# Four pipelined loops of a two-layer transformer kernel written out in full

## The reference, cut to what matters

```python
# layer 0 (per sequence; cond gives scale and shift)
h = film(rmsnorm(x, norm1_w), cond, film1_w, film1_b)
Q, K, V = h @ q_w + q_b, h @ k_w + k_b, h @ v_w + v_b          # one head, 256 wide
x = x + softmax(Q @ K.T * 256**-0.5) @ V @ proj_w + proj_b
h = film(rmsnorm(x, norm2_w), cond, film2_w, film2_b)
x = x + gelu(h @ mlp_w1 + mlp_b1) @ mlp_w2 + mlp_b2             # 256 -> 1024 -> 256
# layer 1
cmod = silu(c) @ w_ada + b_ada                                  # six vectors per sequence
k, q, v = split(modulate(ln(x)) @ w_qkv)                        # 16 heads of 16 channels
x = x + gate_msa * (softmax(q @ k.T / 16) @ v @ w_proj + b_proj)
x = x + gate_mlp * (gelu(modulate(ln(x)) @ w_mlp1 + b_mlp1) @ w_mlp2 + b_mlp2)
```

## Time and profile before

| | |
|---|---|
| timed runs, median (lowest to highest) | 1570.15 us (1569.04 to 1573.56) |
| profiled execution / its span | 1573.3 / 1571.3 us |
| PE busy | 97% of the span, 14186 matmuls |
| weight loads (PEld) | 87% |
| DVE, ACT, POOL busy | 81%, 57%, 32% |
| granted TensorE clock, mean | 0.995 of full speed |
| DMA | 148.55 MB, mean 95 GB/s |
| chain that ended last | PE 78%, DVE 8%, SPq 7%, DMA 3%, issue 2% |

### The profile page before, as it was taken

The page is one execution under the profiler, slowest core; times in us unless marked ns, Lnnn a source line. Parts: engine busy times, 40 slices in busy tenths (PEclk is TensorE's granted clock), DMA queues, the critical chain, the costliest instruction groups (busy, mean ns, idle before and its releaser), DMA issues.

```text
span 1571.3 us, 42207 instructions
## 1 busy us (share of the span) xinstructions
PE 1518.1 (97%) x14186; PEld 1361.8 (87%) x14186; DVE 1275.0 (81%) x2826; ACT 891.7 (57%) x1813; POOL 499.5 (32%) x647
## 2 busy tenths in 40 slices
PE   8999999999999998899999999999998999999999
PEld 7999998999999998666777777777766999999999
DVE  5798888787777778788888888888885888888886
ACT  3566664444444453677777777777777344444443
POOL 2333332010000013366655666655644300000000
PEclk9999999999999999999999999999999999999999
DMA  5700002211111111444444434434432233232332
GB/s 177 220 21 20 20 20 63 77 43 48 46 53 47 47 50 54 142 132 133 140 132 133 137 130 134 141 127 138 133 117 75 80 99 101 93 95 93 100 100 68
DMA packets 167663, 148.55 MB, mean 95 GB/s; under 512 B 24528, under 2 KB 146448, under 8 KB 167584
## 3 DMA queue, kind: packets, MB, share of 16 engines
q1 hardware_dynamic: 167424, 147.47, 29.6%
q0 software_dynamic: 160, 0.04, 0.1%
HBM read 62.61 MB, written 32.41 MB: 60 GB/s over the span
## 4 chain that ended last, share of the span: by engine, by line
PE 78%; DVE 8%; SPq 7%; DMA 3%; issue 2%; ACT 1%; DVEq 0%; ACTq 0%
PE bank L216 60%; PE bank L1755 6%; SPq L1695 4%; DVE C_negmax L1767 4%; PE bank L1793 3%; PE bank L1811 3%; SPq L2118 2%; DMA C_qs<-C_mT 2%; PE bank L1821 2%; PE bank L1829 1%; PE bank L415 1%; PE bank L793 1%; PE bank L488 1%; SPq L287 1%; PE bank L198 1%
## 5 line engine op out<-in xcount | busy, mean ns | idle before, releaser
L1767 DVE TENSOR_REDUCE C_negmax<-bank 128x4 f32<-128x1024 f32 x248 | 303.3, 1223 | 75.4 <-PE bank L1755 74.5
L1901 ACT ACTIVATE C_probs<-bank 128x1024 f32<-128x1024 f32 x256 | 262.5, 1025 | 111.3 <-PE bank L1793 106.7
L374 POOL TENSOR_TENSOR m_small<-m_small,consts 128x2 f32<-128x2 f32 x64 | 48.2, 753 | 573.9 <-DVE m_small L368 290.3
L1129 ACT ACTIVATE B_g<-bank,B_bias 128x256 f32<-128x256 f32 x256 | 107.4, 471 | 196.7 <-PE bank L216 196.4
L1129 ACT ACTIVATE D_g<-bank,D_bias 128x256 f32<-128x256 f32 x256 | 107.3, 472 | 190.9 <-PE bank L216 190.7
L1755 PEld LDWEIGHTS bank<-C_kx,C_qs 64*128 64x128 f32 x1024 | 80.8, 193 | 90.0 <-DVE C_negmax L1767 60.5
L1755 PE MATMUL bank<-C_kx,C_qs 64*128 64x256 f32 x1024 | 128.2, 328 | 21.5 <-DMA C_qs<-C_q_lo 8.0
L216 PE MATMUL bank<-B_wt_w_hi,B_g_lo 128*128 128x256 f32 x512 | 143.0, 279 | 3.5 <-DVE B_g_lo L1139 3.4
L216 PE MATMUL bank<-D_wt_w_hi,D_g_lo 128*128 128x256 f32 x512 | 142.3, 278 | 3.3 <-DVE D_g_lo L1139 3.3
L216 PE MATMUL bank<-D_wt_w_lo,D_g_hi 128*128 128x256 f32 x512 | 141.8, 277 | 0.0
L216 PE MATMUL bank<-D_wt_w_hi,D_g_hi 128*128 128x256 f32 x512 | 141.8, 277 | 0.0
(11 more groups left out here) (270 smaller groups left out, 4909.2 us busy)
## 6 DMA issues: line engine op xcount, KB each, us to landing
C_qs<-C_q_hi SPq DMA_DIRECT2D x128, 128.0 KB
C_kx<-C_k_hi SPq DMA_DIRECT2D x128, 128.0 KB, 2.5
C_qs<-C_q_lo SPq DMA_DIRECT2D x64, 128.0 KB
C_kx<-C_k_lo SPq DMA_DIRECT2D x64, 128.0 KB, 2.6
C_gbc<-mod_rows SPq DMA_DIRECT2D x32, 256.0 KB, 4.0
D_gbc<-mod_rows SPq DMA_DIRECT2D x32, 256.0 KB, 3.4
turned<-N_blocks SPq DMA_DIRECT2D x31, 256.0 KB, 2.0
N_back<-turned SPq DMA_DIRECT2D x124, 64.0 KB, 2.0
```

The costliest lines, as they stand in the source:

```text
L374: self.e_rstd.by(eng.tensor_tensor(self.rstd[:, :], self.var[:, :], neghalf[:, :], ALU.pow))
L1129: ins = eng.activation(o, p, func, bias=per_seq(bias1, 2 * u + d, b))
L1767: e_max.by(eng.tensor_reduce(m4[:, :, :, j], spair[:, :].rearrange("p (e q k) -> p e q k", e=2, q=TH), AX, ALU.max, negate=True))
L1901: e_exp.by(eng.activation(probs[t % NP][:, :], stpair[:, :], ACT.Exp, scale=scl))
```

## The change

`run_pipeline` no longer opens a hardware loop. All iterations of all four phases on all five engines are written out one after another, with plain numbers:

```diff
 def run_pipeline(eng, n_seq, max_skew, iteration, first=0, tail=0):
 
-    for i in range(first, PEEL):
-        iteration(Seq(None, i))
-    with eng.Fori(PEEL // UNROLL, (n_seq - tail) // UNROLL) as j:
-        for u in range(UNROLL):
-            iteration(Seq(j, u))
-    for i in range(n_seq - tail, n_seq + max_skew):
+    for i in range(first, n_seq + max_skew):
         iteration(Seq(None, i))
```

## The result

The changed kernel takes 1588.29 us in the median of four runs (1579.71, 1586.33, 1590.25, 1590.35), against 1571.86 for the kernel before: slower by a factor of 1.0094, 95% interval 1.0049 to 1.0138. Forecast was slower, 1576, with a range up to 1581. The direction was right, the size was not, and the spread of the four runs is part of the answer. The profiled execution is the fastest of the four: 1579.71 us, span 1577.9. In a later set of ten runs beside the same kernel before it took 1582.15 (1579.81 to 1587.61) against 1574.94: a factor of 1.0044, interval 1.0028 to 1.0060.

A forecast was written before the change was run, and what follows sets the result against it. PE, busy 97% of the span, was taken as the bound, with phase C hanging on DVE maxima, SP, DMA, PE. C +7.5, A -1.3, B and D nothing: +6.2 on 1570.15 us, about 1576, range 1568 to 1581.

The forecast's parts named there:

- Phase D and B, nothing: Phases B and D: no change, since PE's queue of matmuls hides branches and register work; D's pair stays 21.76 us.
- Phase C, +7.5 us: Phase C: instruction packets stretch SP's issues, so the maxima's DMAs go out later; ten pairs lose 7.5 us, bounds 0 to 21.
- Phase A, -1.3 us: Phase A: wait and register instruction ahead of each pass's first `A_q_hi` go, saving 0.12 us in 11 passes, 1.3 us less.
- The sum, 1579.5: Whole kernel: 7.5 - 1.3 = +6.2 us on the profiled execution of 1573.3 us.
- rival 1: Phase C: about half the packets drift into SP's idle stretches, +2.7 us, so 1573 us; chance 0.20.
- Rival 2: Phase C: its slow start is only settling, fast afterwards in either form; only A's gain remains, 1569 us; chance 0.12.
- rival 3: All 41 passes: PE pays for branches and register waits; removing them gives 8.5 us, about 1562 us; chance 0.06.
- Rival 4: Phases B and D: fetches cost there too, 0.4 us in each of 19 pairs, +7.6 more, 1584 us; chance 0.06.

The follow-up runs named there:

- the five traces: Traces with phase C full of q8 packets: the changed kernel twice, only C written out, only PE's C loop written out, PE's C loop with ten-iteration passes.
- C alone: Only phase C's loops written out, A, B and D still looped, against the kernel before: 1578.94 us, ratio 1.0048.
- a body of ten: Kernel before, all looped, but PE's loop in phase C has two passes of ten iterations instead of eleven of two: 1583.80 us, ratio 1.0068.

## Where the prediction was right and where it was wrong

**Phase D and B, nothing: right.** D's pair is 21.75 against 21.76; B as a whole takes 0.5 us more, D 0.1.

**Phase C, +7.5 us: the size of a pair right, the path half right.** The packets of q8 run all through C, every long issue of SP coincides with one, and these 22 sequences of C take 8.3 us more, 0.75 a pair where 0.79 had been read. But the prediction knew one path only (SP issues in order, so the maxima's DMAs go out later) and named PE's wait for `C_qs<-C_mT` as the one that grows. It fell from 4.6 to 1.7 us; the wait for `C_qs<-C_q_lo` is new in this window, 6.1 us, and more than half of such waits in the five traces is late landing and not late issue. The prediction took the earlier trace rows as bearing out a hold-up of the data by a packet; they show the issue alone, 0.66 us longer, and it is the changed kernel's semaphore updates that show data held up, by 2.1 us for a packet of 1.5.

What the forecast called one price is in fact two of opposite sign, and the experiments part them. Over the same 22 sequences a pair takes 36.11 before, 35.42 with SP's loop alone written out, 35.59 with all but PE's loop, 36.93 with PE's loop alone and 36.86 with everything. So the packets cost 0.8 us a pair beside a looped SP (36.93 - 36.11) and 1.3 beside a written-out one (36.86 - 35.59), and writing out SP's loop gives 0.7 back without packets (36.11 - 35.42) and next to nothing with them (36.93 - 36.86): the two prices do not simply add. I had this gain inside my number, since the written-out pair of the earlier trace rows held it too, but I did not see it: I wrote that the looped form costs nothing where PE is the bound, and looked for the price of register work on PE and ACT, not on SP, whose queue I had just named as what C waits for.

**Phase A, -1.3 us: wrong by most of it.** The 0.48 us after the transposes did become 0.36 in all iterations of the old loop but one, but two sequences of A take 13.00 us in the mean where they took 13.05. It was given back in the next step: the twelve matmuls of the attention product run in 1.40 to 1.44 us in nearly every iteration where most ran in 1.37, with no wait between them. PE's timeline, the first matmul and the one behind the last, changed kernel and then before:

```profile
158.15 0.30 PE L211 MATMUL bank<-A_v_hi,A_pT_lo 128*128 128x256 f32 x1
...
159.59 0.28 PE L211 MATMUL bank<-a_h_hi,A_m_lo 128*128 128x256 f32 x1
```

```profile
159.18 0.28 PE L216 MATMUL bank<-A_v_hi,A_pT_lo 128*128 128x256 f32 x1
...
160.54 0.28 PE L216 MATMUL bank<-a_h_hi,A_m_lo 128*128 128x256 f32 x1
```

Why they run slower was not tried. The kernel with A, B and D written out shows no gain either.

**The sum, 1579.5 against 1579.7 in the profiled execution: near by luck.** By the traces the span grew by 6.6 us: 0.75 less before A's first result, nothing in A, 0.5 more in B, 6.7 in C as a whole (8.3 over the 22 sequences, 1.4 less at its end) and 0.1 after it. The two savings were in no sum: the kernel before had a half-clock stretch of 3.4 us at 19 us and one at 1224 us, at the end of C, and this execution of the changed kernel has neither. It has two others, at 654 and 1043 us, so that both traces hold the same 17 us at half clock. A's missing gain and these savings come close to cancelling.

**The step that failed: the clock, put at nothing.** The sum and the range carry every cost over from one execution at a mean clock of 0.995, and have no term for the clock. The four timed runs have mean clocks of 0.995, 0.991, 0.988 and 0.990 at 1579.7, 1586.3, 1590.3 and 1590.4 us: at 0.995 the forecast holds, below it the time leaves the range. A mean lower by 0.007 over 1590 us is 22 us more at half clock, between six and seven stretches of 3.4, worth up to 11 us; the third run is 10.5 us longer than the first. So the excess over the forecast is of the size that the clock accounts for.

What the record shows of its cause is less. In the traces a stretch can follow a late landing: the pair around 1043 us lost 2.6 us where PE's idle alone was 1.88. The changed kernel has two stretches between 640 and 1220 us in each of its two traces (at 654 and 1043, and at 659 and 1178) where the kernel before has none. But the length of an idle does not decide: over all thirteen traces, in that part of C, PE has 23 idles of 1.5 us or more; 8 of them, of 1.74 to 2.21 us, were followed by a stretch, and 15, of up to 2.03 us, were not. One of each, PE's loop alone and C alone:

```profile
839.76 0.55 PE L1768 MATMUL bank<-C_kx,C_qs 64*128 64x256 f32 x4 [1.97 <-DMA C_qs<-C_q_lo]
```

```profile
799.62 0.52 PE L1768 MATMUL bank<-C_kx,C_qs 64*128 64x256 f32 x4 [1.99 <-DMA C_qs<-C_q_lo]
```

And the spread is not the changed kernel's alone: of 67 timed runs of the kernel before beside the experiments, the 5 at a clock of 0.997 take 1569.4 us in the mean and the 7 at 0.992 take 1577.6. The tie is loose, too: one of the ten later runs of the changed kernel takes 1585.9 at 0.995. That the stretches of the three long runs were caused by packets is not shown, since these runs have no trace.

Ten more runs in a later set gave 1.0044, which is the forecast's ratio (1576.35 / 1570.15 = 1.0039), so the middle of the forecast fits a typical execution, with the luck in its parts, and the first set was a bad one. What makes a set of executions good or bad stays open.

**The rivals.** The drift of packets (rival 1) is real: the pace wanders between 36.2 and 37.8 over some ten iterations. But its mean, 0.75 over the loop's pace, is the price of the pair that I had read, not half of it. Rival 2 (a slow start) is refuted by the pace in C after the 12th iteration; rival 3 (PE's branches) by D, whose pair did not change when they went; its sum came near to another thing by chance: with the packets kept away, taking SP's loop of C out is worth 7 us, and all loops but PE's in C 8. The page "Runtime: NRT & Kernel Launch" of the Trainium skill, section "Instruction fetch mechanics", calls the cost of straight code mostly hidden; in A, B and D it is, and in C, where another queue on the same DMA engines is critical, it is not. Rival 4 is refuted by D's 21.75 and by the kernel with A, B and D written out.

## What to carry to other kernels

Writing a loop out moves code into the DMA engines' traffic. Where PE waits for DMAs that have just been issued, keep PE's loop, whose stream is the longest by far, short enough that no packets run during it, and write out the loop of the issuing engine, whose register work stands in the queue. Ask of each engine by itself what its loop costs and what its straight code costs; here the two answers differed between engines, and the best kernel mixes them. When a DMA is late, look whether it was issued late or landed late: the two look alike in PE's wait, and a view of the issues shows only the first. And read the mean clock of every timed run before a range is set on one profile.

## What the runs showed of the hardware that had not been expected

- An instruction packet of q8 holds up both the issuing queue and the data. In the changed kernel SP's issue of a DMA took up to 1.88 us with one in flight, against 0.60 in the median, and a DMA issued on time had its sixteenth update 3.6 us after the issue in place of 1.5, with the other fifteen on time.
- The smaller packets of q14 (8 KB against 16) mostly pass unseen, 19 of them in C at a pair of 35.3 to 35.7 us; but with DVE's or ACT's loop alone one of them stood beside a landing that was 0.8 to 0.9 us late.
- A branch of PE's sequencer took 208 ns over a body of two iterations and 3398 ns over a body of ten, of which PE showed 1.57 us as idle.
- Some 20 register instructions a pair of iterations on SP, 1.0 us by their durations, cost 0.7 to 0.8 us a pair: little in that queue is free when it is the bound.
- In the kernel with A, B and D written out, the looped phase C ran at 35.9 us a pair in place of 36.1, with the same code. This is not explained.
